# Reordering GpSimd's list of a step in a fused gated-linear-attention and mixture-of-experts layer

## The reference

```python
xn = layernorm(x)
x = x + attention(xn) + experts(xn)

# attention: 4 heads, keys of 32, values of 64, chunks of 64 tokens, decay g = log_sigmoid(xn @ Wgk + bgk) / 16
A = (q @ k^T) * exp(gc_t - gc_s) for s <= t, else 0      # q scaled by 32 ** -0.5; gc is the running sum of g
o = A @ v + (q * exp(gc)) @ S                            # S: the decayed sum of k v^T of the chunks before
o = o * rsqrt(mean(o * o) + 1e-5) * gnorm_w * silu(xn @ Wg)
attention = o @ Wo

# experts: 8, one for each token, chosen by argmax of softmax(xn @ gate_w)
y = gelu(xn @ w1[e] + b1[e]) @ w2[e] + b2[e]
experts = y * softmax probability of e
```

## Time and profile before

| | us |
|---|---|
| median of 3 runs | 436.49 (435.81 to 437.33) |
| the profiled execution | 436.22 |
| its span | 434.4 |
| TensorE busy | 389.0 (90%) |
| VectorE busy | 326.3 (75%) |
| ScalarE busy | 310.0 (71%) |
| GpSimd busy | 297.1 (68%) |
| 64 scatters into `sorted_rows` | 73.0 |
| 32 masks | 35.6 |
| 32 powers | 53.3 |

### The profile page before, as it was taken

The page is one execution under the profiler, slowest core; times in us unless marked ns, Lnnn a source line. Parts: engine busy times, 40 slices in busy tenths (PEclk is TensorE's granted clock), DMA queues, the critical chain, the costliest instruction groups (busy, mean ns, idle before and its releaser), DMA issues.

```text
span 434.4 us, 13589 instructions
## 1 busy us (share of the span) xinstructions
PE 389.0 (90%) x3650; PEld 336.6 (77%) x3651; DVE 326.3 (75%) x930; ACT 310.0 (71%) x949; POOL 297.1 (68%) x245
## 2 busy tenths in 40 slices
PE   6866889989989899898998999989999999999990
PEld 5645678877767777676776777879999999999990
DVE  5977798988788778778778777866776876767660
ACT  4769888886877868778678687746666766666660
POOL 7532253357878778788787874328888888888884
PEclk9989999999999999999999999999999999999996
DMA  8726489435445343364453424015554555555530
GB/s 239 200 63 194 143 240 314 139 107 172 147 135 182 96 139 116 127 174 136 149 176 119 147 101 129 26 38 69 68 72 61 68 63 64 70 69 67 68 36 0
DMA packets 59098, 51.30 MB, mean 118 GB/s; under 512 B 7201, under 2 KB 51393, under 8 KB 59073
## 3 DMA queue, kind: packets, MB, share of 16 engines
q1 hardware_dynamic: 45936, 42.07, 33.2%
q0 software_dynamic: 12272, 8.54, 14.1%
q10 hardware_dynamic: 864, 0.40, 0.4%
HBM read 33.14 MB, written 18.30 MB: 118 GB/s over the span
## 4 chain that ended last, share of the span: by engine, by line
PE 52%; DVE 13%; issue 11%; ACT 11%; POOL 8%; DMA 1%; DVEq 1%; ACTq 1%; SPq 0%; POOLq 0%
PE psA L905 15%; PE psVG L893 14%; ACT E L1067 6%; PE psVG L722 5%; PE psA L735 4%; DVE msn L1384 4%; POOL sorted_rows L550 4%; PE psQK L710 3%; POOL rms L544 3%; PE psT L780 3%; PE psO L754 2%; DVE stats L1221 2%; ACT sq L1076 2%; PE psT L788 1%; DMA x_all<-in_L_attn_x_dram 1%
## 5 line engine op out<-in xcount | busy, mean ns | idle before, releaser
L584 POOL DMA_INDIRECT out_dram<-yw,sidx x71 | 115.0, 1619 | 29.1 <-issue 11.3
L550 POOL DMA_INDIRECT sorted_rows<-x_all,pos_i x64 | 73.0, 1140 | 35.3 <-PE psT L780 26.3
L1067 ACT ACTIVATE E<-gcB,ngc 128x128 f32<-128x128 f32 x256 | 78.6, 403 | 0.0
L537 POOL TENSOR_SCALAR_AFFINE_SELECT E<-E 128x1024 f32<-128x1024 f32 x32 | 35.6, 1111 | 41.7 <-ACT E L1067 41.4
L544 POOL TENSOR_TENSOR rms<-msn,neg_half 128x8 f32<-128x8 f32 x32 | 53.3, 1664 | 9.2 <-DVE msn L1384 8.5
L1040 ACT ACTIVATE qb<-psQK,qmask 128x256 f32<-128x256 f32 x64 | 26.9, 474 | 38.7 <-PE psQK L710 35.8
L1412 DVE TENSOR_TENSOR pr<-psA,E 128x512 f32<-128x512 f32 x64 | 41.0, 682 | 16.7 <-POOL E L537 16.6
L754 PEld LDWEIGHTS psO<-v_sb,pr 128*64 128x64 f32 x1024 | 38.2, 137 | 18.3 <-issue 11.6
L754 PE MATMUL psO<-v_sb,pr 128*64 128x64 f32 x1024 | 42.3, 225 | 8.1 <-DVE og L1424 5.4
L905 PE MATMUL psA<-xT_all,v_sb 128*128 x288 | 38.3, 276 | 0.4 <-issue 0.4
L893 PE MATMUL psVG<-xgT,gcB 128*128 128x128 f32 x288 | 38.6, 277 | 0.0
(11 more groups left out here) (191 smaller groups left out, 944.4 us busy)
## 6 DMA issues: line engine op xcount, KB each, us to landing
gcB<-decay_rows SPq DMA_DIRECT2D x32, 512.0 KB
sorted_rows<-blank SPq DMA_DIRECT2D x12, 396.0 KB, 5.3
xg<-sorted_rows SPq DMA_DIRECT2D x71, 66.0 KB
x_all<-in_L_attn_x_dram SPq DMA_DIRECT2D x16, 256.0 KB, 5.4
out_dram<-res SPq DMA_DIRECT2D x32, 128.0 KB
eqB<-decay_exp_rows SPq DMA_DIRECT2D x32, 64.0 KB
w1b<-in_L_ffn_w_dram SPq DMA_DIRECT2D x8, 256.0 KB
xT_all<-in_L_ffn_w_dram SPq DMA_DIRECT2D x32, 64.0 KB
```

Of the source, the lines that this page charges most:

```text
L537: nc.gpsimd.affine_select(out=E[j][:], in_=E[j][:], pattern=[[0, 2 * H], [1, P]], compare_op=ALU.is_ge, fill=0.0, base=0, channel_multipli ...
L550: nc.gpsimd.indirect_dma_start(out=sorted_dram, out_offset=bass.IndirectOffsetOnAxis(ap=pos_i[:, t:t + 1], axis=0), in_=x_all[:, t, :], in ...
L584: nc.gpsimd.indirect_dma_start(out=out_rows, out_offset=bass.IndirectOffsetOnAxis(ap=sidx[j][:], axis=0), in_=yw[j][:], in_offset=None, bo ...
L1067: last = nc.scalar.activation(E[j][:, k, h * P:(h + 1) * P], gcB[j][:, k * H + h, :], ACT.Exp, bias=ngcf[:, bass.ds((s * 2 + k) * H + h, 1)])
```

## The change

GpSimd's list of a step is put in another order, and its two waits for TensorE are exchanged. The power comes directly behind the mask. Two scatters follow behind a wait for the state of this step (`s_ready`), and one behind a wait for the outputs of this step (`o_ready`). The rows scattered in each step stay the same, and so does every other engine's list.

```diff
@@ -557,18 +557,17 @@
                 if s == PLACE_FROM:
                     pool.wait_ge(dve_late, LATE)
                     pool.wait_ge(sort_cleared, CLEARS * 16)
-                if s >= PLACE_FROM and t < TILES:
-                    pool.wait_ge(qk_ready, s + 2)
-                    place_rows(t)
                 if s >= 1:
                     if s >= 2:
                         pool.wait_ge(dve_on, s - 1)
                     rms_step(*divmod(s - 1, 2))
                 if s == 2:
                     finish_band()
-                if s >= PLACE_FROM and t + 1 < TILES:
+                if s >= PLACE_FROM and t < TILES:
+                    pool.wait_ge(s_ready, s + 1)
+                    place_rows(t)
                     place_rows(t + 1)
-                    pool.wait_ge(oT_ps_ready, s)
+                    pool.wait_ge(o_ready, s + 1)
                     place_rows(t + 2)
```

## The result

The changed kernel takes 442.38 us (median of 4, 441.79 to 444.51) beside 436.43 (435.81 to 437.33) of the kernel before on the same chip: a ratio (of the means) of 1.0144, with a 95% interval of 1.0104 to 1.0183. It is slower by more than the noise, and by less than 2%. The profiled execution took 441.79, its span 440.0. The forecast of 416.8 was wrong in sign, and the time lies outside its range.

What follows compares the result with a forecast made beforehand. GpSimd's exchanges with TensorE were taken to cost 21.6 us in steps 7 to 28. The sum 21 x 6.95 + 7.6 = 153.55 against 173.24 saves 19.7 us, giving 416.8 us, range 414.5 to 427.

Steps and rivals of the forecast that it cites:

- ring (a): Loop from outputs via third scatter, mask, `pr` and `og` to the next outputs: 6.63 us, under TensorE's 6.90 by 0.27.
- The third scatter* waits for the outputs: +6.47 + 0.82: Third scatter starts 0.82 us after the outputs' end, at +7.29 after kT at the earliest, and takes 0.96.
- rival 3: Outputs' report to third scatter takes over 2.05 us, making it slower; at 2.5, period 8.3 and 446 us; chance 0.06.
- The back-to-back gap: Second scatter directly behind the first on GpSimd: a gap of 0.18 us, then 0.97 for the scatter.
- TensorE's own 6.89: TensorE's step without a wait, from kT to the next kT, taken as +6.90 us from step 29.
- The stretch of the first scatter: First scatter takes 1.50 us instead of 0.97 if `on` has just begun: between +0 and +0.53.
- the alternation that it causes: A stretched scatter delays the next mask, leaving the next scatter unstretched; every second step loses about 0.11, period 6.95 us.
- The 10 us of cover behind step 29: Last placing scatter comes about 2 us later, hidden because the expert stage reads sorted rows more than 10 us on.
- Half of the cast in step 8: VectorE's block-table cast takes 1.27 us; between nothing and 1.27 reaches TensorE, half taken, 7.6 us for the step.
- Rival 1: Back-to-back scatters cost what the expert stage's do, 1.86 us from one to the next; 419.5 to 433, chance 0.12.
- Rival 2: `on` is held by the two scatters: 7.5 us a step, 428; by the first alone 7.3, 424; chance 0.16.
- Rival 4: Nothing changes: GpSimd remains the bound at its present pace, as `on` didn't wait for the power; 436 us, chance 0.04.

Runs made afterwards that it cites:

- the kernel before (433.70): Kernel before with one edit: the third scatter waits for the outputs instead of the transposes; 433.70 us, ratio 0.9958.
- without it (441.88): Changed kernel's order with the two waits of the kernel before (q/k projection, transpose), so no wait for the outputs; 441.88 us, ratio 1.0148.
- kernel at 415.30: Changed kernel without the wait for the state ahead of the first scatter, the raise between the scatters kept; 415.30 us, ratio 0.9533.
- kernel without held reports: Changed kernel without the semaphore raise ahead of the second scatter, so TensorE's reports arrive promptly; 422.63 us, ratio 0.9668.
- the forecast's own kernel: Changed kernel without the semaphore raise ahead of the second scatter; 422.63 us, ratio 0.9668.

## Why the prediction was wrong

**The step that failed** is a term of ring (a): "*The third scatter* waits for the outputs: +6.47 + 0.82". The term between the outputs' end and the third scatter measures 2.37 in step 21, and with it ring (a) is 6.63 - 0.82 + 2.37 = 8.18, beside 8.16 measured on average over 20 steps (163.16 / 20). The prediction had this as rival 3, with its point (2.05) and its price (8.3 at 2.5, 446 us) sized well, and with a chance of 0.06. But rival 3 blamed the wait for the outputs itself, and that isn't the cause: the same wait is prompt in the kernel before (433.70), and the report is late without it (441.88). I took 0.82 as the price of any waited-for scatter because the 21 of before agree. None of them had the combination that the change introduces: a scatter whose raise carries a wait, a second raise, a second scatter. The second scatter was costed by what it costs GpSimd, between 0.17 + 0.98 and 0.30 + 1.56; what it does to another engine's report had no row and was put at nothing without a reason.

**What the runs showed in its place.** Three things together hold TensorE's reports, and with any one of them gone no report is held, but for the one of step 7 in the kernel without the second scatter, 0.48 us late, for which no run has a cause: a wait on the first scatter's raise (without: 415.30), a raise between the scatters (without: 422.63; moved ahead of both: 420.24), a second scatter directly behind it (without: 416.09; with a 0.12 us instruction between: 422.26, though its `memset` isn't tried without the other). With all three at this place of the step it is 441.65 to 442.50 in five kernels, whatever the waits are for; with the second held off by 1.22 us the three are met by the next pair, and 20 other reports are late (430.69). That is shown. Why the chip does it is open: the semaphore record puts the second raise ahead of the first scatter's start (207.64 and 208.11 here), but it does so in the undisturbed kernel at 415.30 as well (201.96 and 203.30), so this doesn't tell them apart.

**The back-to-back gap** was a term of the wrong size: 0.18 forecast, 0.30 measured, both behind the first and behind the second. With the second at 1.08 for 0.97 in a stretched step and the first at 1.52 for 1.45, the third scatter of such a step doesn't start at +7.67 but at +8.11 (213.87, with kT at 205.76), and every second step loses 0.57 instead of 0.11. In the kernel without held reports a pair of steps takes 6.89 + 7.47 = 14.36 where the forecast had 13.90: 20 steps are 4.6 us more, and step 8 took 8.19 for 7.6. Together 416.8 + 5.2 = 422.0, beside 422.63 measured. So of the 25.6 us by which the changed kernel misses the forecast 19.8 are held reports and 5.8 this.

**Right:** TensorE's own 6.89, reached in step 7 and, from step 9 on, in every step of four experiments. The power ends 2.97 after the mask's start (204.94 to 207.91; forecast 2.98), `on` starts at +3.39 (3.4), the outputs at +3.28 (3.26). The stretch of the first scatter where `on` began just ahead of it (by 0.48 to 0.56) and the alternation that it causes, both in the kernels without held reports. The 10 us of cover behind step 29: steps 29 and 30 take 13.78, for 13.79, and what is behind them takes 158.9 us for 159.0. Half of the cast in step 8 was a choice between two bounds and no finding: 7.6 was forecast, 7.73 is what the kernel at 415.30 takes, but 8.19 the forecast's own kernel and 8.54 the changed one.

**Rivals 1, 2 and 4.** Rival 1 (the pair costs what the experts' scatters do): 1.34 from one to the next, not 1.86, so no. Rival 2 (`on` held by the scatters): no; `on` begins 0.22 behind the first scatter (208.33 after 208.11) and takes its 0.68, here and wherever else it begins 0.06 or more behind one; begun within 0.02 of the start, it took 0.70 to 0.73 in the kernel with both raises ahead. The prediction took from the Trainium skill ("SBUF — State Buffer", Who interferes with whom) that `on` would wait for the scatter's end. That holds only if a scatter counts as an instruction that reads SBUF. The section doesn't say so; it says that a `tensor_tensor` was not seen to stall a GpSimd transfer, and infers that making the transfer's descriptors needs the shared port's write side, where a `tensor_tensor` takes only its read side. The 0.68 agrees with that. The stretch to 1.44 to 1.53 us of a scatter that `on` began 0.05 to 0.15 ahead of doesn't, and the measurement decides. Rival 4 (nothing): no; in the kernel without held reports the new order was worth 13.6 us (436.22 to 422.63) of the 19.7 forecast.

**The waits as such.** The wait for the state ahead of the first scatter was a cost even without held reports: 422.63 with it, 415.14 without. It pushes the first scatter to +4.89, where `on` has just begun and stretches it, and the pair then runs into the third. Without it the first starts at +4.5, ahead of `on` at +4.75, and takes 1.03. The forecast never asked what the wait was good for; with that line taken out the kernel takes 0.9533 of before, level with the one that also lacks the raise (0.9540), and these two are the fastest here that sort all rows. TensorE is then busy without a break in each step from 9 on.

## What to carry to other kernels

When a change puts two instructions in a row that no row of the profile shows in a row, its cost has two parts: their time on their own engine, and what they do to the reports of the others. Look for the second in the trace as waits of several engines that end together, with a releaser that isn't an instruction. Ahead of a GpSimd transfer try the kernel without every wait that orders nothing, a satisfied one too, and measure a pair of transfers with and without the semaphore instruction between.

## What was new about the hardware

- TensorE's reports were up to 1.95 us late and arrived together when they fell due beside the second of two indirect transfers on GpSimd 0.30 us apart, where the first's raise carried a wait and a raise stood between. At the turn from step 21 to 22 three due at 209.80, 210.38 and 210.51 arrived 0.96 to 1.05 us after that transfer's end; in the changed kernel's 21 steps the outputs' came 0.79 to 1.03 after it.
- A wait that is satisfied long before cost 26.4 us over the 21 steps with such a pair (415.30 to 441.65), and a bare raise 19.8 us (422.63 to 442.38). The same raise cost nothing without the wait (415.14 and 415.30).
- Two indirect transfers of 128 rows stood 0.30 us apart, whether a raise, no raise or a 0.12 us `memset` was between them. One for which GpSimd stood idle waiting for TensorE started 0.82 us after the transposes' end in all 21 steps of the kernel before, and 0.83 after the outputs' end in 20 of 21 steps at 415.30.
- `msn`, begun inside a scatter with the mask queued behind, again ended with the mask: 1.35 us instead of 0.17 (204.74 to 206.09, the mask to 206.05), as in the earlier trace rows.
